# Two halved transfers of x, another order of the early products, and x queued behind a step's pieces, in a graph layer with an 8192 x 8192 matrix

## The reference

```python
def _L0_gnn_ref(x, adj, W, b):
    support = jnp.matmul(x, W)
    out = jnp.matmul(adj, support) + b
    return jax.nn.relu(out)
h = jnp.maximum(_layernorm(x, axis=-1), 0.0)
x = x + _L0_gnn_ref(h, adj, L0_gnn_W, L0_gnn_b)
return x
```

## Time and profile before

| | us |
|---|---|
| median of 3 runs | 722.26 |
| the three runs | 722.26, 723.55, 722.25 |
| the profiled execution's own time | 723.28 |
| its span, first to last instruction | 721.4 |
| PE busy in the span | 715.2 |
| DVE busy | 621.9 |
| ACT busy | 517.9 |

### The profile page before, as it was taken

How to read it: one execution, slowest core, us unless ns; L and a number is a source line. 1 busy time by engine, 2 the same in 40 slices (tenths; PEclk the granted TensorE clock), 3 DMA queues, 4 the chain that set the end, 5 groups by cost and what they waited for, 6 DMA issues and landing times.

```text
span 721.4 us, 7905 instructions
## 1 busy us (share of the span) xinstructions
PE 715.2 (99%) x3113; PEld 584.3 (81%) x3113; DVE 621.9 (86%) x394; ACT 517.9 (72%) x400; POOL 173.3 (24%) x99
## 2 busy tenths in 40 slices
PE   8999999999999999999999999999999999999998
PEld 3788888888888888888888888888888888888886
DVE  5999999999999888988798888878888787888886
ACT  1888898888888867766677667666676666777562
POOL 3544455555444401432041000000000000021022
PEclk9999999999999999999999999999999999999999
DMA  8999999999999999999999999999999999999992
GB/s 352 407 408 408 408 412 416 412 416 415 417 415 417 414 401 401 412 387 399 366 416 429 367 403 400 375 394 380 389 397 375 385 387 382 404 405 405 361 391 87
DMA packets 45109, 281.60 MB, mean 390 GB/s; under 512 B 5136, under 2 KB 5776, under 8 KB 31504
## 3 DMA queue, kind: packets, MB, share of 16 engines
q1 hardware_dynamic: 44496, 280.25, 97.1%
q10 hardware_dynamic: 576, 0.85, 0.3%
HBM read 276.89 MB, written 4.19 MB: 390 GB/s over the span
## 4 chain that ended last, share of the span: by engine, by line
PE 95%; DMA 3%; SPq 1%; DVE 0%; ACT 0%; issue 0%; DVEq 0%
PE banks L583 93%; DMA raw<-adj 3%; PE banks L610 0%; PE banks L611 0%; PE banks L609 0%; SPq L268 0%; DVE low L541 0%; ACT high L402 0%; SPq L265 0%; DVE x_sb L503 0%; DVE x_sb L511 0%; DVEq L173 0%; SPq L283 0%; DVEq L502 0%
## 5 line engine op out<-in xcount | busy, mean ns | idle before, releaser
L541 DVE TENSOR_TENSOR low<-raw,high 128x3072 fp32r<-128x3072 f32 (+3 forms) x261 | 575.8, 2231 | 84.6 <-PE banks L583 68.4
L402 ACT ACTIVATE high<-raw 128x3072 fp32r<-128x3072 f32 (+3 forms) x261 | 483.8, 1864 | 191.0 <-DMA raw<-adj 165.1
L583 PE MATMUL banks<-high,h_high 128*128 128x512 f32 x1012 | 272.6, 390 | 0.3 <-ACT high L402 0.3
L583 PE MATMUL banks<-high,h_low 128*128 128x512 f32 x1012 | 271.9, 389 | 0.0
L583 PE MATMUL banks<-low,h_high 128*128 128x512 f32 x1012 | 268.7, 389 | 0.0
L583 PEld LDWEIGHTS banks<-high,h_high 128*128 128x128 f32 x1012 | 189.8, 188 | 41.1 <-ACT high L402 1.4
L583 PEld LDWEIGHTS banks<-low,h_high 128*128 128x128 f32 x1012 | 189.8, 188 | 39.8 <-DVE low L541 0.6
L583 PEld LDWEIGHTS banks<-high,h_low 128*128 128x128 f32 x1012 | 190.0, 188 | 39.5
L354 POOL TENSOR_SCALAR x_sb<-x_sb,bias 128x512 f32<-128x512 f32 x16 | 53.5, 3348 | 415.7 <-DMA x_sb<-x_blocks 415.7
L345 POOL TENSOR_SCALAR z_sb<-x_sb,neg_mean,rstd 128x128 f32<-128x128 f32 x60 | 87.7, 1474 | 1.6
L330 POOL TENSOR_TENSOR rstd<-var_eps,minus_half 128x4 f32<-128x4 f32 (+2 forms) x17 | 31.5, 1853 | 121.3 <-DVE var_eps L445 110.5
(11 more groups left out here) (34 smaller groups left out, 47.9 us busy)
## 6 DMA issues: line engine op xcount, KB each, us to landing
raw<-adj SPq DMA_DIRECT2D x106, 1536.0 KB, 8.5
raw<-adj SPq DMA_DIRECT2D x82, 768.0 KB, 11.0
raw<-adj SPq DMA_DIRECT2D x69, 512.0 KB, 11.9
x_sb<-x_blocks SPq DMA_DIRECT2D x16, 256.0 KB, 8.2
out_blocks<-x_sb SPq DMA_DIRECT2D x15, 256.0 KB, 9.2
x_sb<-x SPq DMA_DIRECT2D x14, 256.0 KB, 12.0
raw<-adj SPq DMA_DIRECT2D x3, 256.0 KB, 7.9
raw<-adj ACTq DMA_DIRECT2D x1, 256.0 KB, 2.9
```

Source lines behind the costliest of these rows:

```text
L402: nc.scalar.activation(high[:, t % HIGH_SLOTS, cols], raw[:, t % RAW_SLOTS, cols], ACT.Copy).then_inc(high_ready, 1)
L541: nc.vector.tensor_tensor(low[:, t % LOW_SLOTS, cols], raw[:, t % RAW_SLOTS, cols], high[:, t % HIGH_SLOTS, cols].bitcast(F32), ALU.subtra ...
L583: return nc.tensor.matmul(banks[:, FIRST_BANK[g] + c, :], h[:, (t - FIRST_STEP[g]) * DEPTHS[g] + k, :], tile[:, slot, at:at + BANK], start ...
```

## The change

It has three pieces.

1. **Order of products.** In steps 2, 3, 10 and 11 (three parts) each part's low products follow its own high products. In steps 4 to 9 (four parts) only part 0 does so; then come the high products of parts 1, 2 and 3, and the low products of 1, 2 and 3 at the end. From step 12 on nothing is changed.
2. **x behind the pieces.** `load_x` of a step is now issued behind the pieces of that step, for all 13 batches from 4 on. Its place moves behind the wait on `low_ready` that the pieces have.
3. **Two transfers for two batches.** Batches 4 and 5 (tiles 12 to 19), loaded at steps 6 and 10, come as one transfer of rows 0 to 87 and one of rows 88 to 127. Both count on the same semaphore, and the awaited count is raised to match.

```diff
+LOW_AT_ONCE_UNTIL = 12
+UNEVEN = range(4, 6)
+ROWS = [range(0, 88), range(88, P)]
...
-                sp.dma_start(x_sb[:, x_slot(j), :], x_batches[j]).then_inc(x_landed[x_slot(j)], 16)
+                for rows in ROWS if j in UNEVEN else [range(P)]:
+                    at = slice(rows[0], rows[-1] + 1)
+                    sp.dma_start(x_sb[at, x_slot(j), :], x_batches[j][at, :]).then_inc(x_landed[x_slot(j)], 16)
...
-                if mean_at(t) is not None:
-                    load_x(mean_at(t))
...
                 for i in range(len(split_of(t))):
                     load_piece(t, i)
+                if mean_at(t) is not None:
+                    load_x(mean_at(t))
...
-                with_high(0)
                 if len(parts) <= 2:
-                    with_low(0)
-                for part in range(1, len(parts)):
-                    with_high(part)
-                    if len(parts) > 2:
+                    for part in range(len(parts)):
+                        with_high(part)
+                        with_low(part)
+                elif t < LOW_AT_ONCE_UNTIL:
+                    for part in range(len(parts)):
+                        with_high(part)
+                        if part == 0 or len(parts) == 3:
+                            with_low(part)
+                    if len(parts) > 3:
+                        for part in range(1, len(parts)):
+                            with_low(part)
+                else:
+                    with_high(0)
+                    for part in range(1, len(parts)):
+                        with_high(part)
                         with_low(part - 1)
-                if len(parts) >= 2:
                     with_low(len(parts) - 1)
```

More of the change, by code:

```diff
@@ L254, in x_landed_count @@
         def x_landed_count(j):
-            return 16 * len([i for i in range(1, j + 1) if x_slot(i) == x_slot(j)])
+            return 16 * sum(len(ROWS) if i in UNEVEN else 1 for i in range(1, j + 1) if x_slot(i) == x_slot(j))
         @block.sync
```

## The result

The changed kernel takes 724.65 us (median of 8 runs, 723.62 to 725.17); the kernel before takes 722.12 (8 runs, 721.91 to 723.55). The ratio is 1.0033 with a 95% interval of 1.0024 to 1.0042: slower by 2.5 us. That is a third of a per cent and would be called the same wherever only 2% counts, but the interval leaves 1 out. The prediction was 722.1, in a range that ended at 723.2.

The account below looks back on a forecast made before the run. PE was taken as the bound, a queue of fixed length; -0.62 + 0.20 + 0.08 + 0.27 - 0.10 = -0.17 us took the profiled 723.28 to 723.1, and the median's 1.02 lower level gave 722.1, range 721.5 to 723.2.

Parts of the forecast that it names:

- What is hidden: Loading of x: two further issues on SP, 0.43 us each, and later landings of x, taken as nothing.
- the last engine is loaded: Rival on the split batches: landings later by 0.32 us a batch, range's upper end 723.2; chance 0.25.
- the last engine is spared: Rival on the split batches: landings earlier by up to 0.64 us, range's lower end 721.5; chance 0.27.
- Step 3: PE waits for part 0's low product under the new order: +0.20 us (0.15 to 0.26).
- Step 6: PE's largest gap, ahead of the second piece's high products, goes away: -0.62 us.
- the small rival on that gap: Rival: step 6's gap isn't in the timed runs, so no gain and 722.5 us; chance 0.08.
- Step 7: PE waits for the first low product: +0.08 us with x moved, 0.60 with x left in place.
- Step 8: PE waits for the first low product, DVE being held by ACT: +0.27 us, taking nearly all the remaining gain.
- Step 11: First low product, behind a sum of x that comes earlier: no wait of PE, nothing.
- From step 12 on: Old order; in step 34 the first low comes earlier because step 33's sum of x does: -0.10 us.
- Slower by a wait of DVE for x: Rival: DVE's sum waits for late x, delaying the next step's lows at 13 batches, about 724.2 us; chance 0.04.
- PE gaps beyond 1 us in sum: Sign that the prediction is wrong: PE's gaps behind step 2 adding to more than 1 us.

Follow-up runs that it names:

- e4_no_split: The changed kernel with batches 4 and 5 of x each in one whole transfer; 722.05 us, 1.0001 of the kernel before.
- e3_split: The kernel before with only batches 4 and 5 in two transfers of 88 and 40 rows, x ahead of the pieces; 724.86 us, 1.0036.
- g3_before: The kernel before, unchanged, run again for a second trace; its profiled execution took 721.93 us.
- g1_rows_0_63: The kernel before with only rows 0 to 63 of batches 4 and 5 loaded, in one transfer, other rows left out; 722.35 us, 1.0007.
- g4_after: The changed kernel, unchanged, run again for a second trace; its profiled execution took 723.89 us.
- after: The changed kernel with all three pieces, against the kernel before; 724.65 us, 1.0033.
- f1_64_64: The kernel before with batches 4 and 5 in two transfers of 64 rows each, old order, x ahead of the pieces; 723.41 us, 1.0021.
- f3_88_alone: The kernel before with only rows 0 to 87 of batches 4 and 5 loaded, in one transfer, other rows left out; 723.07 us, 1.0015.
- f4_40_alone: The kernel before with only rows 88 to 127 of batches 4 and 5 loaded, in one transfer, other rows left out; 722.14 us, 1.0001.
- g2_rows_32_95: The kernel before with only rows 32 to 95 of batches 4 and 5 loaded, in one transfer, other rows left out; 721.53 us, 0.9993.
- e1_order: The kernel before with only the new order of products, x whole and ahead of the pieces; 722.36 us, 1.0004.
- e2_x_behind: The kernel before with only x moved behind the pieces, old order, x in one transfer; 721.79 us, 0.9995.

## Why the prediction was wrong

**The step that failed** is "What is hidden": the split of batches 4 and 5 was "taken as nothing". It costs 2.4 us (the changed kernel against e4_no_split) and 2.9 by itself (e3_split), and it cost 1.4 even with two halves of 64 rows. The prediction did see that no row shows how such a transfer is spread over engines, and its range rests on that: the upper end, 723.2, on a term of 0.32 us a batch for landings that are later (*the last engine is loaded*), the lower, 721.5, on up to 0.64 for landings that are earlier (*the last engine is spared*). No run shows either term; what the runs showed in their place is about 1.0 us of lost rate a batch in the changed kernel. The load was the wrong quantity. It asks how many bytes each engine carries and takes the rate at which an engine carries them as given; the rate itself falls while such a transfer is under way (249 GB/s in place of 405 in e3_split).

Little hides it. The transfers are a full resource, the pieces behind x are late by what x takes longer, and PE had only one small gap to give (0.53 in g3_before). So a delay of the DMA at steps 6 and 10 passes on to PE, and from there to the end. What it costs depends on how late PE is already. In the profiled execution of g1_rows_0_63 PE began step 2 at 17.78, where it began at 15.70 in g3_before, while the last piece ahead of batch 4 landed at 28.2 and 28.1 in the mean of its sixteen events. In spite of 1.0 us of lost rate its weight loads then didn't wait once between 20 and 60 us.

**How far the sizes go.** The rates are those of one profiled execution, and the last column but one is PE's loss in that same execution: the time from its first matmul of step 5 to its first of step 14, less the 37.19 of g3_before. The last column is from the medians (g4_after is a single execution).

| run | lost rate, both batches | bytes left out | sum | PE's loss in the same trace | measured over before |
|---|---|---|---|---|---|
| after | 2.0 | | 2.0 | 1.0 | 2.5 |
| g4_after | 2.2 | | 2.2 | 2.1 | 2.0 |
| e3_split | 2.3 | | 2.3 | 2.9 | 2.9 |
| f1_64_64 | 2.5 | | 2.5 | 2.5 | 1.4 |
| f3_88_alone | 0.9 | -0.4 | 0.5 | 0.8 | 1.1 |
| f4_40_alone | 1.0 | -0.9 | 0.1 | -0.4 | 0.1 |
| g1_rows_0_63 | 1.0 | -0.6 | 0.4 | -0.5 | 0.45 |
| g2_rows_32_95 | 0 | -0.6 | -0.6 | -0.5 | -0.4 |

Trace and median are of different executions, and some are far apart. The profiled one of f1_64_64 was the longest of its eleven (724.91, 2.9 over before), and in it 2.5 us of lost rate went with 2.5 us of lost PE time; why the others were shorter no trace shows. That of `after` was the shortest of its eight, and nearly all of its 1.0 was lost from step 9 on. At batch 4 its first piece of step 7 was complete at 35.59, by its last engine, and in e4_no_split at 35.76: there two engines were more than 1 us behind the other fourteen without any split, which hides what the split does to those. In f4_40_alone PE lost 0.5 only later, between step 14 and the first product with W (225.26 us in place of 224.74).

e3_split lost 0.6 more than its lost rate. An uneven load could fill that by an estimate: a batch in one transfer takes 0.64 us at 408 GB/s, and engines with twelve rows of x in place of eight would be late by half of it, 0.32 a batch or 0.64 for both. But g4_after has the same load and lost 0.1 less than its lost rate. In f3_88_alone the bytes left out may save nothing, if eleven engines carry as much as ever; then the sum is 0.9, near PE's 0.8. That the load is uneven is seen. A piece's semaphore is raised sixteen times, read here as once by each engine when it is done; for the first piece behind the split batch 4 in e3_split, and the last piece ahead of it, these are the times from the trace's semaphore events:

```
ahead of x   27.81 27.83 27.84 27.88 27.94 28.00 28.02 28.19 28.20 28.29 28.30 28.32 28.39 28.53 28.57 28.59
behind x     30.27 30.28 30.42 30.51 30.66   31.02 31.05 31.06 31.09 31.11 31.13 31.14 31.20 31.33 31.53 31.54
```

Five are early and eleven late. That fits the landings of x in the runs that issue one transfer, eleven for 88 rows in f3_88_alone and ten for 40 rows in f4_40_alone, if the ten are among the eleven. But the five that are early, and by that count carry nothing of x, ended 1.9 to 2.6 us behind the piece ahead in the mean, by which times of the upper row are theirs (1.7 at the least), and a piece of 512 KB takes 1.28 at 408 GB/s. They too are held up, which the load can't do and P would. How the 2.4 us of the changed kernel divide between the lost rate and the uneven load is argued here, not shown: no run has the uneven load without the lost rate. Half the rate would account for 0.32 with 64 rows (128 KB take 0.32 at the full rate, twice that at half), and 0.5 is seen in g1_rows_0_63; the rest, too, is open.

**The rest of the sum**, which stands as e4_no_split now that the split is out of it: -0.17 forecast, +0.1 measured with an interval of -0.6 to +0.7. That can't tell the forecast from nothing, so the terms are read one by one, each from a single trace. (The lower end that the prediction gives, -0.6, is -0.52 by its own terms.)

- *Step 3.* Forecast 0.20. In the changed kernel PE's first low product started at 21.69, 0.64 behind the high products ahead of it in place of 0.45, and the next row started 0.57 later: 0.19 and 0.12, together 0.31, a little above the upper value of 0.26. By the starts of steps 3 and 4 the same wait is 0.28 in e1_order, 0.19 in e4_no_split and 0.01 in g4_after.

```profile
21.05 0.61 PE L590 MATMUL banks<-high,h_low 128*128 128x512 f32 x2
21.69 0.73 PE L590 MATMUL banks<-low,h_high 128*128 128x512 f32 x2
22.26 0.63 PE L590 MATMUL banks<-high,h_high 128*128 128x512 f32 x2
```

- *Step 6.* The gap of the earlier trace rows is gone, as forecast. Two rows of the changed kernel at that place start 0.45 apart:

```profile
34.07 0.62 PE L590 MATMUL banks<-low,h_high 128*128 128x512 f32 x2
34.52 0.61 PE L590 MATMUL banks<-high,h_high 128*128 128x512 f32 x2
```

  Its size was read from one execution that ran longer than most: 0.62 there. In g3_before the same gap is 0.27 and 0.11, 0.38. The gain was oversized by 0.24, which is part of the small rival on that gap. In g4_after step 6 has two other waits, for the single blocks of its last piece (0.26 and 0.22 in the list above).
- *Step 7.* Forecast 0.08 with x moved and 0.60 without. e4_no_split: the start of the low product is 0.12 late and its restart takes 0.11, 0.23. e1_order: 0.60. So moving x does pay for the order, as worked out, though not all of it.
- *Step 8.* Forecast 0.27, "the term on which the result hangs". e4_no_split: 0.08 and 0.11, 0.19. Right in place and near in size.
- *Step 11.* Forecast nothing. In e4_no_split there is none. In g4_after the waits of 54.51 and 55.84 (0.71 and 0.57 of idle weight loads) are among the largest, behind the second split batch.
- *From step 12 on.* Forecast a gain of 0.10. From PE's first matmul of step 14 to the first product with W g3_before takes 224.74 and e4_no_split 224.47, but e1_order, in which x isn't moved, 224.41. A gain from moving x isn't shown.
- *Slower by a wait of DVE for x.* False as a mechanism, though the kernel did get slower: in the traces of the changed kernel DVE never waited for x (16 to 60 us in the first, 20 to 300 in the second). In the first the last of batch 4 landed at 34.56, 0.77 behind the last of the piece ahead of it (33.79), and that of the piece behind it at 35.59, in order of issue. Its sum of batch 4, in g4_after, follows the lows of step 6 without idle time, while its lows now wait for ACT, and ACT for a piece:

```profile
34.63 1.30 DVE L548 TENSOR_TENSOR low<-raw,high 128x512 fp32r<-128x512 f32 x2 [1.29 <-ACT high L409]
35.84 0.68 DVE L441 TENSOR_REDUCE neg_sum<-x_sb 128x4 f32<-128x512 f32 x1
36.56 0.17 DVE L446 TENSOR_SCALAR neg_mean<-neg_sum 128x4 f32<-128x4 f32 x1
37.03 3.56 DVE L548 TENSOR_TENSOR low<-raw,high 128x1024 fp32r<-128x1024 f32 x4 [0.30 <-ACT high L409]
```

The signs that the prediction named for itself were the right ones to look at and one of them fired: PE gaps beyond 1 us in sum. The 0.93 for "no change" was too sure. Within 2% it came true, but the prediction's own cases for it all lay within 0.2% of before, and the loss is 0.33%. It held three costs of the split (issue, load, landing) to be all there could be, though no row of the kernel before shows a transfer of other than 128 rows, and it left the rate out of the bounds.

None of the experiments beats the kernel before by more than can be told; e2_x_behind (0.9995, 0.9986 to 1.0004) comes nearest among those that leave nothing out.

## What to carry to other kernels

Cut a load into the SBUF by columns rather than by rows, or leave it whole: by columns the cut was free here, by rows (88 and 40, or 64 and 64) it cost 1.0 to 1.4 us of the full rate for each 256 KB. If a transfer must have fewer rows, it matters which: 32 to 95 ran at the full rate and 0 to 63 didn't. Where the DMA queue is full, ask of each changed transfer at what rate it will run and not only how many bytes each engine gets: in e3_split 1.0 us was lost while batch 4 was under way, and the first piece behind it landed last at 31.54, where it did at 30.43 in g3_before. And read the rate in GB/s in fine slices beside the DMA's busy share: the share stood at 1.03 while the rate fell from 405 to 354.

## What the runs showed of the hardware

- While a transfer of 64 rows of 2 KB was under way, all transfers together ran at about half the rate (217 GB/s in the mean of five slices of 0.2 us) when it went into rows 0 to 63, and at the full rate when it went into rows 32 to 95 (412 in the mean of the same five).
- The slowing isn't confined to the transfer that causes it: in e3_split the five earliest landings of the piece behind x, which by their count are those of the engines that carry nothing of it, came 1.9 to 2.6 us in the mean behind their landings of the piece ahead, where a piece takes 1.28 at 408 GB/s.
- Rows of 1 KB instead of 2 KB, in two transfers that each span 128 rows, cost nothing that can be told (1.0001, 0.9993 to 1.0010; 398 and 406 GB/s).
- Two executions of the kernel before differ by 1.3 us in their spans (721.4 and 720.1), and it arose early: PE was alone from 35.14 in one and from 33.63 in the other. That is half of what this change costs. A difference of that size between two traces is not yet one between two kernels. The two 64-row kernels show it again: 1.98 of the 2.0 us between their traces stood before the rows in which they differ were loaded.
